# Row maxima of the second attention run one and a half groups ahead of the scores in place of two

## The reference

```python
q = (x @ Wq).reshape(b, n, N_HEADS, HEAD_DIM)       # 32 heads of 16
k, v = jnp.split(ctx @ Wkv, 2, axis=-1)
q = apply_axial_rope(q, pos_map); k = apply_axial_rope(k, ctx_pos_map)
logits = jnp.einsum('bqhd,bkhd->bhqk', q, k) * scale
w = jax.nn.softmax(logits, axis=-1)
attn = jnp.einsum('bhqk,bkhd->bqhd', w, v)
```

## Time and profile before

| | |
|---|---|
| median of 3 runs | 1950.35 us (1949.76 to 1953.46) |
| the profiled execution's own time | 1947.62 us |
| its span, from the first to the last instruction | 1945.8 us |
| mean granted TensorE clock | 0.937 of full speed |
| busy share: TensorE, VectorE, ScalarE, GpSimd | 88%, 59%, 41%, 22% |
| the second attention | from 678 to 1132 us of the span |

### The profile page before, as it was taken

How to read it: one execution, slowest core, us unless ns; L and a number is a source line. 1 busy time by engine, 2 the same in 40 slices (tenths; PEclk the granted TensorE clock), 3 DMA queues, 4 the chain that set the end, 5 groups by cost and what they waited for, 6 DMA issues and landing times. The chain is left out here.

```text
span 1945.8 us, 29323 instructions
## 1 busy us (share of the span) xinstructions
PE 1712.5 (88%) x8787; PEld 1295.1 (67%) x8787; DVE 1151.0 (59%) x2061; ACT 799.3 (41%) x1264; POOL 422.7 (22%) x384
## 2 busy tenths in 40 slices
PE   6987799999486569999999987899999968999997
PEld 5776699999365435555555555677877746787785
DVE  5876522222487368888888735555545555555555
ACT  5553232322333226666666743333333324333332
POOL 1210122322445670000000000222222203222221
PEclk9998799999687769999999998999999979999999
DMA  8993146631579743333333101011011030101101
GB/s 300 340 339 132 39 166 234 224 138 62 202 255 307 252 116 87 75 84 89 78 78 89 46 0 37 21 41 41 21 40 40 1 85 21 41 21 40 40 20 44
DMA packets 171935, 208.54 MB, mean 107 GB/s; under 512 B 61424, under 2 KB 114672, under 8 KB 166976
## 3 DMA queue, kind: packets, MB, share of 16 engines
q1 hardware_dynamic: 165456, 186.34, 31.4%
q0 software_dynamic: 6384, 20.98, 3.2%
HBM read 262.33 MB, written 78.51 MB: 175 GB/s over the span
## 5 line engine op out<-in xcount | busy, mean ns | idle before, releaser
L1941 DVE TENSOR_REDUCE r_top<-r_ring 128x1 f32<-128x512 f32 x512 | 330.5, 686 | 42.8 <-PE r_ring L1840 40.5
L1925 ACT ACTIVATE r_probs<-r_st 128x1024 f32<-128x1024 f32 x256 | 248.3, 1022 | 132.6 <-PE r_st L1829 129.4
L2502 POOL TENSOR_TENSOR f_hidS<-f_work,f_hidS 128x512 fp32r<-128x512 f32 x132 | 170.5, 1292 | 415.9 <-ACT f_hidS L2462 415.9
L1840 PE MATMUL r_ring<-r_kM,r_qS 128*128 128x512 f32 x512 | 207.2, 447 | 36.4 <-DMA r_v<-v_pad 33.6
L1840 PEld LDWEIGHTS r_ring<-r_kM,r_qS 128*128 128x128 f32 x512 | 99.8, 196 | 123.5 <-DVE r_top L1941 69.4
L48 PE MATMUL m_bank<-w_place,m_xT 128*128 x936 | 166.0, 326 | 4.4 <-DVE m_xT L1189 3.1
L2619 DVE TENSOR_TENSOR f_work<-f_work,f_u 128x512 f32<-128x512 f32 x132 | 90.8, 688 | 132.3 <-PE f_u L48 74.0
L1829 PE MATMUL r_st<-r_qS,r_kM 128*128 128x512 f32 x512 | 160.7, 397 | 0.0
L48 PEld LDWEIGHTS m_bank<-w_place,m_xT 128*128 128x128 f32 x936 | 151.3, 189 | 8.6 <-issue 5.3
L2457 ACT ACTIVATE f_work<-f_g 128x512 f32<-128x512 f32 x132 | 78.9, 598 | 181.8 <-PE f_g L56 124.7
L2462 ACT ACTIVATE f_hidS<-f_work 128x512 fp32r<-128x512 f32 x132 | 83.3, 631 | 168.7 <-DVE f_work L2619 168.7
(11 more groups left out here) (344 smaller groups left out, 2851.7 us busy)
## 6 DMA issues: line engine op xcount, KB each, us to landing
w_place<-expert_split SPq DMA_DIRECT2D x72, 1408.0 KB
w_place<-expert_split SPq DMA_DIRECT2D x36, 1024.0 KB
expert_split<-w_place SPq DMA_DIRECT2D x10, 1408.0 KB, 8.8
w_place<-expert_split SPq DMA_DIRECT2D x36, 384.0 KB
r_qS<-q_stack SPq DMA_DIRECT2D x64, 200.0 KB
k_stack<-q_qk SPq DMA_DIRECT2D x48, 256.0 KB, 4.1
q_stack<-q_qk SPq DMA_DIRECT2D x48, 256.0 KB, 3.7
r_kM<-k_stack SPq DMA_DIRECT2D x64, 192.0 KB
```

Source lines behind the costliest of these rows:

```text
L1840: nc.tensor.matmul(ring(place(q, h))[:], qS[s][:, h // 2, q * P:(q + 1) * P], kM[s][:, h, :], start=True, stop=True).then_inc(max_ready, 1)
L1925: nc.scalar.activation(probs[k][:, 2 * pair:2 * pair + 2, :], st_ps[pair][:], ACT.Exp, scale=SCALE).then_inc(exp_done, 1)
L1941: nc.vector.reduce_max(top[s % 2][:, q, h:h + 1], ring(place(q, h))[:], AXIS_X).then_inc(max_read, 1)
L2502: nc.gpsimd.tensor_tensor(hidS[c][:, var, LO, :], hid(c, var), fp32(hidS[c][:, var, HI, :]), ALU.subtract).then_inc(hid_split, 1)
```

## The change

The maxima run one and a half groups ahead of the scores. Before the first step, the maxima of group 0 and only the tiles 0 and 1 of group 1 are formed. In step g, the quarters k = 0 and 1 take tiles 2 and 3 of group g+1, and k = 2 and 3 take tiles 0 and 1 of group g+2. The work that hangs on the maxima moves along with them: VectorE makes the shifts of group g+1 after quarter 1 of step g, TensorE turns them after the values of quarter 2 and ScalarE copies them after the exponentials of quarter 2; the output of group g-1 is turned in quarter 3 and normalised there. The order of the ring places stays the same. The code of SyncE isn't edited.

```diff
+        ahead = [(0, q) for q in range(KT)] + [(1, q) for q in range(KT // 2)]
...
-            for g in range(2):
-                for q in range(KT):
-                    maxima(g, 0, g, q, range(GROUP))
-                    if (g, q) == (1, 0):
-                        turn_shifts(0, 0)
+            for g, q in ahead:
+                maxima(g, 0, g, q, range(GROUP))
+                if (g, q) == (1, 0):
+                    turn_shifts(0, 0)
...
                     def maxima_of(*heads):
-                        if left >= 2:
-                            maxima(g + 2, i + (s + 2) // RING, (s + 2) % RING, k, heads)
+                        on = 1 + (k >= KT // 2)
+                        if left >= on:
+                            maxima(g + on, i + (s + on) // RING, (s + on) % RING, (k + KT // 2) % KT, heads)
...
                     if k == 0:
                         if not first:
                             values(g - 1, (s - 1) % RING, KT - 1)
-                        if left >= 1:
-                            turn_shifts(g + 1, (s + 1) % RING)
                     else:
                         values(g, s, k - 1)
-                        if k == 1 and not first:
+                        if k == KT // 2 and left >= 1:
+                            turn_shifts(g + 1, (s + 1) % RING)
+                        if k == KT // 2 + 1 and not first:
                             turn_out(g - 1)
...
-                    if k == 0:
-                        if not first:
-                            copy_out(g - 1)
-                        if left >= 1:
-                            copy_shifts(g + 1, (s + 1) % RING)
+                    if k == 0 and not first:
+                        copy_out(g - 1)
+                    if k == KT // 2 and left >= 1:
+                        copy_shifts(g + 1, (s + 1) % RING)
...
-            for g in range(2):
-                for q in range(KT):
-                    read_maxima(g, g, q)
-                make_shifts(g)
+            for g, q in ahead:
+                read_maxima(g, g, q)
+                if q == KT - 1:
+                    make_shifts(g)
...
-                for q in range(KT):
-                    if left >= 2:
-                        read_maxima(g + 2, s, q)
-                    if q == 1 and not first:
+                for k in range(KT):
+                    on = 1 + (k >= KT // 2)
+                    if left >= on:
+                        read_maxima(g + on, (s + on) % RING, (k + KT // 2) % KT)
+                    if k == KT // 2 - 1 and left >= 1:
+                        make_shifts((s + 1) % RING)
+                    if k == KT // 2 + 1 and not first:
                         normalise(g - 1)
-                if left >= 2:
-                    make_shifts((s + 2) % RING)
```

## The result

The changed kernel takes 1968.96 us, the median of 4 runs (1964.67 to 1980.43), against 1950.35 before (1949.76 to 1953.46). The ratio is 1.0101, with a 95% interval of 1.0057 to 1.0145: slower by 1%, where 1966.9 us had been forecast.

What follows compares the result with a forecast made beforehand. TensorE's stream was taken to bound the second attention. A start gain of 6.1 us, 0.65 us more per step and a longer end left it 16.5 us behind: 1950.35 + 16.5 = 1966.9 us, range 1955 to 1978.

Steps and rivals of the forecast that it cites:

- The chain: Second attention, shift transposes, copy, four DMAs, first scores: 4.75 us (4.38 to 5.05) needed, 3.90 us covering it.
- The period: One steady step of the second attention: 13.76 us against 13.11 before, 0.65 us more in each step.
- the remainder: From the load of a step's first scores to the next shift transposes: three quarters less 0.11, 9.01 us.
- The start: Up to the first scores of step 1: eight maxima less before step 0, 6.1 us gained.
- make_shifts costs nothing in its new place: VectorE's making of the shifts, now between quarters 1 and 2: same place among the ring's banks, no added time.
- Steps and end: Steps 1 to 29 leave the kernel 13.0 us behind at step 30; step 30 makes it 16.5 in all.
- the unchanged code: Phases after the attention: they start later and aren't changed, so no time was added for them.
- The hidden chain: Rival for the attention's steps: no step waits for the shifts, 5.0 us faster, 1945.3 us; chance 8%.
- Its condition: For no step to wait, the time from shift transposes to next first scores must be at most 3.90 us.
- The clock rival: Rival for the attention's steps: TensorE's wait lets its clock fall, 46 us on top, about 2013 us; chance 5%.

Runs made afterwards that it cites:

- Experiments 1, 2 and 5: A fifth shift DMA in the changed kernel: 1990.83 us; the same in the kernel before: 1952.71 us; changed kernel with a semaphore per pair of heads: 1952.02 us.
- experiment 4: The changed kernel with two of the four shift DMAs issued from ScalarE's queue instead of SyncE's: 1952.10 us, ratio 0.9998.

## Why the prediction was right

**The chain.** Forecast 4.75 us, measured 4.81 in step 1: the transposes until the copy 0.64 (forecast 0.63), copy until the first issue 0.61 (0.62), first issue until TensorE goes on 738.51 - 734.95 = 3.56 (3.5, in bounds of 3.13 and 3.8). Over steps 1 to 29 it is 4.90, with 3.65 for the DMAs. Experiments 1, 2 and 5 show that this chain, by its last DMA, sets the step.

**The period.** Forecast 4.75 + 9.01 = 13.76 us, measured 4.90 + 8.88 = 13.78. That the two agree to 0.02 is luck: the chain was 0.15 longer and the remainder 0.13 shorter than reckoned (747.40 - 738.51 = 8.89 in step 1), and in the sum these cancel. The remainder was counted from a load that ran ahead of its matmul, by 0.23 us (854.79 and 855.02); behind the wait both start together (862.57 and 862.58). For the same reason 4.10 us and not 3.90 are covered, counted to the matmul.

**The start.** Forecast 6.1 us gained at the first scores of step 1. Measured: 730.14 before, 724.80 - 1.18 = 723.6 after, 6.5 gained. The load of group 2 ended the wait in quarter 2 as forecast, 0.5 us earlier than before (716.95 - 1.18 = 715.77 against 716.25). But the statement that make_shifts costs nothing in its new place holds for the steady steps alone. In step 0 it now lies on the way to the next transposes, next to GpSimd's additions, and in three of the six profiles with half a group's distance less and the additions in their old place it took 3 us or more, and the transposes of step 0 came some 3 us later. Before, the shifts of group 1 were followed by the wait for the load, which hid them. The forecast had no term for this, and the execution that it was compared with was one of the three in which it cost little.

**Steps and end.** 13.0 us behind at step 30 were forecast and 1124.28 - 1.18 - 1110.11 = 13.0 measured; 16.5 at step 31, and 1137.03 - 1.18 - 1119.50 = 16.4 measured. The attention grew by 16.2. That the median still came out 2.1 us above the forecast isn't from these terms, as far as the profiles show, but from the unchanged code, which the prediction took to stay as it was.

**The rivals.** The hidden chain, as a forecast, is wrong for this kernel, but it describes experiment 4: 5.0 us were reckoned for it and its attention was 5.8 shorter in one profile. Its condition was too strict by 0.2 us, since that chain is 4.08 and not 3.90 and costs nothing. The clock rival is wrong for the steps: in a window of one step of the changed kernel the granted clock is 1.00, and so it is from 730 to 1120 us in both of its profiles. At the longer wait of step 31 it did come once, for 1.3 us in all.

```profile
733.70:747.40 13.70, 13.15 (x77) 7.00 (x73) 11.47 (x21) 8.94 (x10) 0.00 (x0) 1.00 0.34 81
```

**What is open.** The medians differ by 18.6 us and the profiled executions by 20.4, of which 16.2 are the attention's. The rest took 813.4 to 816.7 us in the four profiles of the kernel before and its variants, and 816.4 to 822.3 in the ten of the others, though its code is the same. In the first two profiles it grew by 3.0 us, 1.4 of them in the first 71 us, up to the feed-forward part. There one part can be read: the first twelve matmuls of the next phase that read the projected weights took 4.22 us before and 5.29 after,

```profile
1138.58 4.22 PE L48 MATMUL o_y<-o_w,o_aT 128*128 128x512 f32 x12
```

```profile
1155.92 5.29 PE L48 MATMUL o_y<-o_w,o_aT 128*128 128x512 f32 x12
```

at a mean granted clock of 0.69 and 0.54 of full speed over that stretch, so the phase met the clock at another moment. The other 1.6 us lie in the feed-forward part, where TensorE was busy for 0.8 us less than before (675.7 against 676.5), so they are idle time; their cause wasn't found.

Whether the rest hangs on the change, the execution or the chip is not settled. On either chip every profile of a variant has a longer rest than those of the kernel before. On the other hand the stretch ahead of the attention, unchanged too, took anything from 688.9 to 695.2 us. It isn't settled either why the total of experiment 4 doesn't show the 5.8 us: the rest was 5.0 longer in its profile, and that profile was one of those in which the first instruction of make_shifts took 0.9 us and not 3 or more, so other executions may well have a longer attention.

## What to carry to other kernels

Before work is moved nearer to its use, measure the whole chain behind it, from the producer's first instruction to the consumer's wait, with the DMAs counted to their landing and not to the end of their issue, and compare it with what will stand between the two. Here 4.9 us had to fit into 4.1, in each of 31 steps, and a gain of 5 us that was reaped once could not pay for that. When the schedule is to stay, shorten the chain at its last link: a second queue, or waiting for just those DMAs that the next instruction reads. Either took the loss away here (1952.10 and 1952.02 us, against 1968.96); a gain over the kernel before was not measured in the total for either.

## What the runs showed of the hardware that was not expected

A VectorE instruction of 0.17 us (tensor_scalar on 128x16, SBUF to SBUF) took 2.96, 4.03 and 4.53 us when it met a series of GpSimd's tensor_tensor on 128x512, and in all three it ended with that series; in other executions of the same code it took 0.3 to 0.9 us for that group. With the additions elsewhere it took 0.17 to 0.18 us in all four profiles. The instruction behind it (scalar_tensor_tensor, which reads two SBUF tiles) took 1.07 to 1.18 us each time that it ran beside the series, in all ten profiles with the additions in their old place, and 0.17 to 0.18 otherwise. The Trainium skill, "GPSIMD Engine Reference", section "Key points", says that GpSimd shares its SBUF interfaces with VectorE, with contention for VectorE's two-port modes or two SBUF inputs. The rows of the second instruction agree; whether the first runs in a two-port mode no run here shows. One of GpSimd's additions takes some 1.24 us (19.79 for 16), so the wait of the first can last over several of them.

Four small DMAs from two queues at once had TensorE loading 867.20 - 864.37 = 2.83 us after the first issue, against 3.64 from one queue (862.57 - 858.93): half the issues on a second queue saved 0.8 us of the 1.2 that they take.
